# Gated cross-attention on one core: the probabilities turned in two row tiles of 64 and 48 queries, with the weighting moved behind later scores

## The reference, cut to what matters

```
x = x + tanh(g0) * cross(layernorm(x), ctx)       # first half, the subject here
x = x + tanh(g1) * switch(layernorm(x))           # second half, unchanged

cross: q = ln(x) @ wq + bq ; k = ctx @ wk + bk ; v = ctx @ wv + bv
       p = softmax(q_h @ k_h.T / 4 + mask * -1e9)   for each of 16 heads of 16 columns
       out = concat_h(p @ v_h) @ wo + bo
```

## Time and profile before

| | |
|---|---|
| median of 3 executions | 1324.6 us (1322.26 to 1331.56) |
| the profiled execution: its time, its span | 1323.86 us, 1322.1 us |
| first half, second half | to about 640 us, from there on |
| busy over the span: TensorE, its weight loads, VectorE, ScalarE, GpSimd | 95%, 77%, 65%, 46%, 42% |
| the group of `turn` (L382) | 1536 matmuls, 170.8 us busy |
| the group of `weigh` (L396) | 3072 matmuls, 101.8 us busy |

### The profile page before, as it was taken

One profiled execution on the slowest core, in us unless ns is written; L12 is line 12 of the kernel. 1 busy time (PEld: TensorE's weight loads), 2 busy tenths in 40 slices (PEclk: granted clock), 3 DMA queues, 4 the chain that ended last, 5 costly groups with the idle time before them and its releaser, 6 DMA issues.

```text
span 1322.1 us, 40356 instructions
## 1 busy us (share of the span) xinstructions
PE 1252.3 (95%) x15928; PEld 1020.8 (77%) x15928; DVE 862.2 (65%) x2455; ACT 613.0 (46%) x1353; POOL 552.1 (42%) x823
## 2 busy tenths in 40 slices
PE   5799999999999999999975999999999999999996
PEld 4577777787778777777654888888888888888885
DVE  2566776776677676667553766776677667766652
ACT  3456555555655655565322443444443344334431
POOL 3476666667667666666510212212221222122211
PEclk9899999999999999999977999999999999999997
DMA  8898897778778767776303666666666556656663
GB/s 230 187 205 183 191 205 164 167 167 181 162 160 190 157 163 178 161 167 145 71 18 84 137 148 146 140 141 150 142 139 143 144 141 141 147 131 143 142 158 89
DMA packets 262975, 200.21 MB, mean 151 GB/s; under 512 B 195906, under 2 KB 243844, under 8 KB 258692
## 3 DMA queue, kind: packets, MB, share of 16 engines
q1 hardware_dynamic: 262788, 197.64, 65.2%
HBM read 125.49 MB, written 72.11 MB: 149 GB/s over the span
## 4 chain that ended last, share of the span: by engine, by line
PE 45%; DMA 3%; DVE 1%; ACT 1%; issue 0%; POOL 0%; POOLq 0%; SPq 0%; ACTq 0%; DVEq 0%
PE bank_ab L996 15%; PE bank_ab L988 4%; PE bank_g L1068 4%; PE bank_s L1044 4%; PE bank_ab L1085 4%; PE bank_g L1078 4%; PE bank_t L1056 3%; PE bank_ab L982 3%; PE bank_g L1032 2%; DMA v_dram<-mv 1%; PE bank_ab L976 1%; DMA pm_dram<-pm 1%; PE bank_t L1068 1%; DMA pm_te<-pm_dram 0%; DMA att_th<-att_dram 0%
## 5 line engine op out<-in xcount | busy, mean ns | idle before, releaser
L753 POOL TENSOR_SCALAR shifted<-raw,neg_max 112x375 f32<-112x375 f32 x512 | 304.7, 603 | 194.2 <-DVE neg_max L646 127.6
L646 DVE CUSTOM_DVE_ANT_0 raw<-bank_s,maskb 112x375 f32<-112x375 f32 x512 | 268.8, 544 | 117.0 <-issue 76.4
L565 ACT ACTIVATE probsT<-bank_t 128x448 f32<-128x448 f32 x384 | 181.1, 546 | 162.7 <-PE bank_t L382 162.7
L382 PE MATMUL bank_t<-ident,shifted 112*128 112x112 f32 x1536 | 170.8, 261 | 2.8 <-POOL shifted L753 2.8
L382 PEld LDWEIGHTS bank_t<-ident,shifted 112*128 112x128 f32 x1536 | 156.1, 141 | 21.5 <-POOL shifted L753 18.6
L373 PE MATMUL bank_s<-K_stack,Q_stack 128*112 128x375 bf16 x512 | 158.6, 337 | 11.9 <-DVE neg_max L646 7.8
L1317 DVE TENSOR_REDUCE max<-bank_s 112x4 f32<-112x448 f32 x128 | 78.7, 615 | 90.2 <-PE bank_s L1044 90.2
L1404 POOL TENSOR_TENSOR mix_bd<-pm_te,tok 128x448 f32<-128x448 f32 x32 | 31.1, 972 | 221.1 <-DMA pm_te<-pm_dram 221.1
L996 PE MATMUL bank_ab<-xnT,wq2T 128*128 128x224 f32 x512 | 111.3, 361 | 0.4 <-ACT xnT L1160 0.4
L996 PE MATMUL bank_ab<-xnT,wk2T 128*128 128x224 f32 x512 | 109.6, 357 | 1.1 <-ACT kT L1189 0.6
L996 PEld LDWEIGHTS bank_ab<-xnT,wq2T 128*128 128x128 f32 x512 | 95.9, 193 | 12.3 <-issue 8.6
(11 more groups left out here) (135 smaller groups left out, 2234.6 us busy)
## 6 DMA issues: line engine op xcount, KB each, us to landing
K_stack<-k_dram SPq DMA_DIRECT2D x64, 562.5 KB, 7.3
k_dram<-k_parts SPq DMA_DIRECT2D x32, 562.5 KB, 4.8
att_dram<-att_q SPq DMA_DIRECT2D x32, 511.0 KB, 4.1
att_th<-att_dram SPq DMA_DIRECT2D x32, 511.0 KB, 4.3
v_dram<-mv SPq DMA_DIRECT2D x32, 455.0 KB, 6.1
v<-v_dram SPq DMA_DIRECT2D x32, 455.0 KB, 4.0
K_stack<-k_dram SPq DMA_DIRECT2D x32, 375.0 KB, 9.3
Q_stack<-q_dram SPq DMA_DIRECT2D x64, 168.0 KB, 9.2
```

Of the source, the lines that this page charges most:

```text
L382: last = nc.tensor.transpose(bank_t[0:KP, k, j * S:(j + 1) * S], shifted[:, g % 2, j, k * KP:(k + 1) * KP], c.ident[0:S, 0:S])
L565: act.activation(probsT[:, g % 2, k, :], bank_t[0:KP, k, 0:G * S], ACT.Exp).then_inc(exp_done, 1)
L646: dve.tensor_tensor_reduce(raw[:, g % 2, j, :], bank_s[h % 2][0:S, 0:S2], c.maskb[:, :], -1.0, -LEAST, ALU.add, ALU.min, neg_max[:, g % 2, ...
L753: pool.tensor_scalar(shifted[:, g % 2, j, 0:S2], raw[:, g % 2, j, :], -1.0, neg_max[:, g % 2, j:j + 1], ALU.mult, ALU.add).then_inc(shift_ ...
```

## The change

`turn` and `exps` of the first half, the layout of `probsT`, and where `weigh` is called.

- Each of the 12 blocks of a group is now transposed by two instructions: rows 0 to 63 (row tile 0 of TensorE) with the 64 x 64 identity, and rows 64 to 111 (the other row tile) with the 48 x 48 identity. The twelve pairs alternate between the two tiles, and the upper half runs two units behind the lower, so that the two never write the same bank at a time (`PLACES`). At unit 8 TensorE waits for its own signal `upper_done`, given at unit 1. The wait for the exponentials of the group before stands ahead of the whole turn, and one signal is given at the end of it, where there were three.
- `exps` waits for the whole turn and has four activations, of 512, 480, 256 and 96 columns, where there were three of 448.
- `weigh` waits for all four, and is called directly ahead of the turn of the next group; weigh 2 is called in the next batch, behind S1.
- On ScalarE `heads_copy` comes behind `key_copy` 0; keys(b+2, 0) comes behind S4 as before, and weigh 3- behind S5.

```diff
--- before.py
+++ after.py
@@ -195,6 +195,13 @@
     NG = H // G
     STACK_LOADS = 16 * 2 * len(STACKED)
     VW = 32
+    UNITS, LOW = KC * G, z.S - 48
+
+
+
+    PLACES = ((0, 8, 0, 0, 0), (0, 10, 1, 1, 0), (8, 12, 0, 2, 0), (10, 12, 1, 2, 4 * LOW))
+    HALVES = ((0, LOW), (LOW, z.S))
+
     with ExitStack() as ctx:
         sb = lambda name, shape, dt=F32: ctx.enter_context(nc.sbuf_tensor(name, shape, dt))
         ps = lambda name, shape: ctx.enter_context(nc.psum_tensor(name, shape, F32))
@@ -210,7 +217,7 @@
         raw = sb("raw", [S, 2, G, S2])
         neg_max = sb("neg_max", [S, 2, G])
         shifted = sb("shifted", [S, 2, G, SK])
-        probsT = sb("probsT", [KP, 2, KC, G * S])
+        probsT = sb("probsT", [KP, 2, UNITS, S])
         headsT = sb("headsT", [P, NG * S])
         recip = sb("recip", [S, H])
         heads = sb("heads", [S, H, D])
@@ -244,6 +251,7 @@
         k_dram = nc.dram_tensor("k_dram", (B, PARTS, E, S2), BF16).ap()
         scores_ready, scores_read, shift_done = sem("scores_ready"), sem("scores_read"), sem("shift_done")
         turned, exp_done, pv_done = sem("turned"), sem("exp_done"), sem("pv_done")
+        upper_done = sem("upper_done")
         headsT_copied, heads_ready, recip_done, heads_done = sem("headsT_copied"), sem("heads_ready"), sem("recip_done"), sem("heads_done")
         outT_ready, outT_copied, y_ready, x_done = sem("outT_ready"), sem("outT_copied"), sem("y_ready"), sem("x_done")
         block = ctx.enter_context(nc.Block())
@@ -375,13 +383,25 @@
 
             def turn(b, g, first):
                 pe.wait_ge(shift_done, H * b + G * g + G)
-                for k in range(KC):
-                    if not (first and g == 0):
-                        pe.wait_ge(exp_done, KC * (NG * b + g - 1) + k + 1)
-                    for j in range(G):
-                        last = nc.tensor.transpose(bank_t[0:KP, k, j * S:(j + 1) * S],
-                                                   shifted[:, g % 2, j, k * KP:(k + 1) * KP], c.ident[0:S, 0:S])
-                    last.then_inc(turned, 1)
+                if not (first and g == 0):
+                    pe.wait_ge(exp_done, len(PLACES) * (NG * b + g))
+
+                def one(half, u):
+                    lo, hi = HALVES[half]
+                    (bank, column), = [(bank, column + (u - first_u) * (hi - lo)) for first_u, end, h, bank, column in PLACES
+                                       if h == half and first_u <= u < end]
+                    k, j = u // G, u % G
+                    return nc.tensor.transpose(bank_t[0:KP, bank, column:column + hi - lo], shifted[lo:hi, g % 2, j, k * KP:(k + 1) * KP], c.ident[lo:hi, lo:hi])
+
+
+                for u in range(UNITS):
+                    if u == 8:
+                        pe.wait_ge(upper_done, NG * b + g + 1)
+                    one(0, u)
+                    last = one(1, (u + UNITS - 2) % UNITS)
+                    if u == 1:
+                        last.then_inc(upper_done, 1)
+                last.then_inc(turned, 1)
 
             def weigh(b, p, g, first):
                 if g == 0:
@@ -390,11 +410,11 @@
                         pe.wait_ge(v_set, 1)
                     else:
                         pe.wait_ge(headsT_copied, b)
+                pe.wait_ge(exp_done, len(PLACES) * (NG * b + g + 1))
                 for k in range(KC):
-                    pe.wait_ge(exp_done, KC * (NG * b + g) + k + 1)
                     for j in range(G):
                         last = nc.tensor.matmul(bank_o[j * VW:(j + 1) * VW, g * S:(g + 1) * S], V[:, p, k, G * g + j, :],
-                                                probsT[:, g % 2, k, j * S:(j + 1) * S], start=(k == 0), stop=(k == KC - 1))
+                                                probsT[:, g % 2, G * k + j, :], start=(k == 0), stop=(k == KC - 1))
                 last.then_inc(pv_done, 1)
 
             def heads_back(b):
@@ -424,27 +444,27 @@
                 S_ = lambda *hs: [scores(b, p, i, h, first) for h in hs]
                 S_(0, 1)
                 if back:
+                    weigh(b - 1, 1 - p, NG - 2, False)
                     turn(b - 1, NG - 1, False)
                 S_(2)
                 if ahead:
                     transposes(b + 2, i + 1, p)
-                S_(3)
+                S_(3, 4)
+                if ahead:
+                    keys(b + 2, p, 0)
+                S_(5)
                 if back:
                     weigh(b - 1, 1 - p, NG - 1, False)
-                S_(4)
-                if ahead:
-                    keys(b + 2, p, 0)
-                S_(5)
                 turn(b, 0, first)
                 S_(6, 7)
                 if ahead:
                     keys(b + 2, p, 1)
-                weigh(b, p, 0, first)
                 if back:
                     if ahead:
                         pe.wait_ge(k_copied, 2 * (EC * (b + 2) + 1))
                     heads_back(b - 1)
                 S_(8)
+                weigh(b, p, 0, first)
                 turn(b, 1, False)
                 S_(9)
                 if ahead:
@@ -455,12 +475,11 @@
                 if front:
                     values(1 - p, 0)
                     values(1 - p, 1).then_inc(va_ready, 1)
-                S_(11)
-                weigh(b, p, 1, False)
-                S_(12)
+                S_(11, 12)
                 if back:
                     project(b - 1)
                 S_(13)
+                weigh(b, p, 1, False)
                 turn(b, 2, False)
                 if ahead:
                     pe.wait_ge(v_copied, 2 * b + 3)
@@ -472,7 +491,6 @@
                     values(1 - p, 2).then_inc(vb_ready, 1)
                 if ahead:
                     queries(b + 2)
-                weigh(b, p, 2, False)
 
             def turn_weights(*numbers):
                 for n in numbers:
@@ -511,6 +529,7 @@
                 pe.wait_ge(wt_copied[n], (len(turns) + 1 - n) // 2)
             pe.wait_ge(v_copied, 2)
             batches(pe, body)
+            weigh(B - 1, 1, NG - 2, False)
             turn(B - 1, NG - 1, False)
             weigh(B - 1, 1, NG - 1, False)
             heads_back(B - 1)
@@ -560,9 +579,11 @@
             def exps(b, g, first):
                 if not (first and g < 2):
                     act.wait_ge(pv_done, NG * b + g - 1)
-                for k in range(KC):
-                    act.wait_ge(turned, KC * (NG * b + g) + k + 1)
-                    act.activation(probsT[:, g % 2, k, :], bank_t[0:KP, k, 0:G * S], ACT.Exp).then_inc(exp_done, 1)
+                act.wait_ge(turned, NG * b + g + 1)
+                for first_u, end, half, bank, column in PLACES:
+                    lo, hi = HALVES[half]
+                    act.activation(probsT[:, g % 2, first_u:end, lo:hi], bank_t[0:KP, bank, column:column + (end - first_u) * (hi - lo)].rearrange("p (u q) -> p u q", q=hi - lo),
+                                   ACT.Exp).then_inc(exp_done, 1)
 
             def heads_copy(b, first):
                 act.wait_ge(pv_done, NG * b + NG)
@@ -582,10 +603,10 @@
                     exps(b - 1, NG - 1, False)
                 if ahead:
                     ctx_copy(b + 2, p, False)
+                if ahead:
+                    key_copy(b + 2, p, i + 1, 0)
                 if not first:
                     heads_copy(b - 1, second)
-                if ahead:
-                    key_copy(b + 2, p, i + 1, 0)
                 exps(b, 0, first)
                 if ahead:
                     key_copy(b + 2, p, i + 1, 1)
@@ -748,7 +769,7 @@
 
                 for j in range(G):
                     h = G * g + j
-                    free = [] if j or (first and g < 2) else [(turned, KC * (NG * b + g - 1))]
+                    free = [] if j or (first and g < 2) else [(turned, NG * b + g - 1)]
                     wait_all(pool, v_set, (scores_read, H * b + h + 1), *free)
                     pool.tensor_scalar(shifted[:, g % 2, j, 0:S2], raw[:, g % 2, j, :], -1.0, neg_max[:, g % 2, j:j + 1],
                                        ALU.mult, ALU.add).then_inc(shift_done, 1)
```

More of the change, by code:

```diff
@@ L430, in body @@
                     transposes(b + 2, i + 1, p)
-                S_(3)
-                if back:
-                    weigh(b - 1, 1 - p, NG - 1, False)
-                S_(4)
+                S_(3, 4)
                 if ahead:
@@ L437, in body @@
                 S_(5)
+                if back:
+                    weigh(b - 1, 1 - p, NG - 1, False)
                 turn(b, 0, first)
```

## The result

The changed kernel took 1346.61 us (median of 4, 1343.17 to 1354.38) against 1324.96 us for the kernel before: ratio 1.016, 95% interval 1.013 to 1.0191. It is slower by some 21 us, about two and a half times the 8 us forecast, and inside the range.

What follows compares the result with a forecast made beforehand. TensorE's queue was taken to bound the first half (98.7% busy). Stretches of 6.16 + 4.40 + 9.19 = 19.75 us a batch instead of 19.46 gave +8 us over 31 batches, 1332 us; range 1308 to 1352.

Steps and rivals of the forecast that it cites:

- The 40 us that TensorE's queue promised: First half: 0.32 us saved a group, 1.28 a batch, some 40 us over 31 batches, if TensorE's queue alone counts.
- the walk through the batch: One batch retraced in the new order with each engine's queue: three stretches, 19.75 us instead of 19.46.
- rival (C): Loop through all four turns decides, dearer terms count four times: at 0.15 a turn +19 us, 1351 us; chance 0.16.
- Twelve pairs give 0.735: New turn on TensorE: twelve transpose pairs at 0.061 us, from the second half's eight in 0.49; 1.15 us before.
- Four pairs more make 0.95: ScalarE's exponentials start 0.95 us behind a turn's start, from 0.70 for the second half's 8 pairs; 0.64 before.
- 0.15 for an exposed weight load: Step from the end of copy_x or ctx_copy to the queries or keys(0): 0.15 us, estimated from loads of 130 to 140 ns.
- 5.28: Stretch score 11 to score 0: the queries can start 5.28 us after score 11, behind copy_x.
- 4.40: Stretch score 0 to keys(0): keys(0) starts 4.40 us after score 0 instead of 3.83, behind ctx_copy.
- Exponentials 1.35: Four exponentials of a group on ScalarE take 1.35 us in all, where three took 1.29; bounds 1.29 and 1.5.
- TensorE is busy about 91%: Sign for the steady part of the first half: TensorE's busy share falls to about 91% from 98.7%.
- (A): TensorE's queue alone counts and the new waits don't come: -1.28 us a batch, 1284 us; chance 0.07.
- (D): Weight loads set the pace, two row tiles don't help: a pair at 0.096 us, turn 1.15, 1383 us; chance 0.04.

Runs made afterwards that it cites:

- e1: Changed kernel with, on ScalarE, ctx_copy ahead of the exponentials of group 3 and copy_x ahead of those of group 2: 19.23 us a batch, ratio 0.9974.
- e3: Kernel before with the calls at the changed places, turn and exponentials in one tile as before: 20.14 us a batch, ratio 1.0201.
- e2: Kernel before with row tiles, one signal and four exponentials as changed, all calls at their old places: 19.78 us a batch, ratio 1.0124.

## Why the prediction was right, and where it was short

The direction and the mechanism held. The 40 us that TensorE's queue promised did not come; a wait for `xnT` appeared ahead of the queries and one for `ctxT` ahead of the keys, each where the walk through the batch had put it; e1 gave the loss back by ScalarE's order alone. The outcome is not the one held most likely, though: "within 1%" had 0.57 and "slower" 0.30, and 1346.61 lies above the forecast's own range of 1320 to 1343. It is inside the whole range of 1308 to 1352 because that takes in most of rival (C).

The size was short, 8 us forecast and 21 measured, by 0.42 us a batch. Taken from the rows of the same batch:

- "Twelve pairs give 0.735": they take about 0.80 (0.90 from the turn's start to the next one, less 0.09 for the emptying). I spread the start of the first pair (some 0.05) over the eight of the earlier trace rows and scaled all of it, but a start is paid once and each pair is dearer. A turn's matmuls cover 0.96 us, of which the last one's length is 0.22, so 12 pairs start over some 0.74, 0.063 a pair without the first start; the second half's 8 pairs by the same reckoning (0.66 less 0.22) 0.056. The moving columns are the same, the stationary ones 128 instead of 112. The bound of 0.066, if the weight loads set the pace, had been named and the lower end taken. 128 to 112 columns would explain the difference, but no run varies them alone, so that the loads set the pace is not shown. The two turns between keys(0) and score 11 make 0.13 us a batch of it.
- "Four pairs more make 0.95": the exponentials start 1.06 and 1.07 behind turns 2 and 3, so `copy_x` and `ctx_copy` come 0.11 and 0.12 later than forecast. About half is the dearer pairs: the turn covers 0.96 us, where 0.66 and four pairs of 0.061 are 0.90. The other half is the step from the turn's end to the exponentials, 0.11 us (325.12 to 325.23) where the second half has 0.04 (913.07 to 913.11); why it is longer here no run shows.
- "0.15 for an exposed weight load": right in sum and wrong in place. From the end of a copy to TensorE it is 0.06; the other 0.1 is inside the group that has waited. So keys(0) take 308.67 - 307.30 = 1.37 instead of 1.26, and the queries 323.04 - 322.06 = 0.98 instead of 0.88. Short windows of the timeline show it, of keys(1), which comes in a running stream, and of keys(0) of the next batch, which has waited:

```profile
310.73 0.35 PEld L348 LDWEIGHTS bank_ab<-ctxT,wk_sb 128*128 128x128 f32 x2
...
310.89 0.48 PE L348 MATMUL bank_ab<-ctxT,wk_sb 128*128 128x375 f32 x1
...
327.46 0.30 PEld L348 LDWEIGHTS bank_ab<-ctxT,wk_sb 128*128 128x128 f32 x2 [0.72 <-ACT ctxT L545]
327.47 0.58 PE L348 MATMUL bank_ab<-ctxT,wk_sb 128*128 128x375 f32 x1 [0.48 <-ACT ctxT L545]
```

In the running stream the first load goes out 0.16 us ahead of its matmul; behind the wait the two start together, and the first matmul lasts 0.58 instead of 0.48. That "5.28" and "4.40" came out as 5.33 and 4.43 is partly luck: the exponentials were 0.1 later and the step behind the copy 0.09 shorter. What was missing shows in the length of the group that has waited.

- In all, the turns make some 0.36 of the 0.42: 0.13 by themselves and 0.23 by the exponentials behind turns 2 and 3. The rest are hundredths, as `ctx_copy` with 0.84 instead of 0.81 and the score ahead of weigh 1, which has waited, with 0.30 instead of 0.26. "Exponentials 1.35" was 1.34; the wait of score 13 came as computed (318.20 - 316.73 = 1.47, forecast 1.48); `upper_done` cost nothing that the trace shows: the pairs start every 0.06 us across it.
- "I forecast 1332: the shorter turn is paid back by ScalarE, whose exponentials start only when the whole turn is done": the summary put it on the row tiles. e3 and e2 say otherwise: the places alone lose 0.71 us a batch, the tiles alone 0.35. The walk had both (turn 3 at 1.14 instead of 0.37 is a place, 2.30 instead of 1.93 behind it is the tiles), the sentence only one.
- Of the signs named, the waits came and were larger: TensorE stands 0.5 us a batch for `ctxT` (its loads 0.8; forecast 0.6) and 0.2 for `xnT` (loads 0.6; forecast 0.3), and the loads 1.4 for `neg_max` (before 0.7). "TensorE is busy about 91%" was 94.0. The share counts the tail of the group ahead of a wait as busy: the score at 326.62 covers 0.37 us, and the row of keys(0) shows 0.48 of waiting, where in a running stream keys(0) would start 0.20 behind the score, 0.65 sooner than it did.

Rival (C), dearer terms counted again and again along the loop, comes closest to what the shortfall was: it added 0.6 us a batch at 0.15 a turn, and of the 0.42 that were missing some 0.36 are the turns', 0.09 each. They came from dearer pairs and a longer step to ScalarE, not from `upper_done`. (A) fell by the two waits; with ScalarE's other order (e1) 0.2 of its 1.28 us shows. (D) is out: 0.063 a pair, not 0.096. The rule of the Trainium skill in "TensorE: Matmul & The Clock Gate", section "LDWEIGHTS (loading the stationary operand)", 107 ns for a load of 128 columns, is not what a pair costs here either. It does fit the 0.1 us that an exposed load adds to a group, and the rows agree that stationary columns count and rows hardly do: 141 and 139 ns for 128 columns with 112 and 64 rows, 132 for 112 columns.

## What to carry to other kernels

A faster step helps only if what waits for it starts sooner too: turning a step with several signals into one with a single signal at the end can take back more than the step saved, because the next engine's queue moves with it. Where an engine works in order, look at what stands behind the delayed work in its queue (here two copies for the next batch): in the changed kernel moving the two copies was worth 0.93 us a batch, and the row tiles, where other queues had been cleared, 0.83. And before a step is moved, follow its result through the transfers to the next user, not only through the engines.

## What had not been expected of the hardware

Two row tiles of 64 and 48 rows ran a pair in 0.063 us with 128 stationary columns and 0.056 with 112, with 64 and 48 moving columns both times. A group that had waited for another engine cost TensorE 0.1 us more than the same group in a running stream, 1.37 against 1.26 us for the four keys matmuls and 0.98 against 0.88 for the eight of the queries: its first weight load, which a running stream sends out ahead, is then in the open.
